# Two buffers instead of one for the layer norm's input and for the output block, in an eight-core transformer kernel

## The chip, the cores and the metric

The kernel runs on the eight cores of one Trainium2 chip. Each core works on 2 of the 16 sequences; no core waits for another or exchanges data with it. The metric is the device time in microseconds (us) of the slowest core. Each core has TensorE (PE; its weight loads are shown apart as PEld), VectorE (DVE), ScalarE (ACT), GpSimd (POOL) and SyncE (SP), which here only issues transfers.

## What is computed

An attention layer with pre-norm, then a feed-forward part that is itself a two-layer transformer with local attention. The edited lines lie in the last part of each of its layers: the norm ahead of `w1`, and the end of the product with `w2`.

```
# x: (16, 2048, 1024) float32
x = x + attention(layernorm(x))
y = layernorm(x)
for l in range(2):
    h = shift_token(y)                       # half of the channels one token later
    y = y + local_attention(h) @ wo[l]
    h = shift_token(y)
    h = (h - mean) / sqrt(var + 1e-5) * ln_g[l] + ln_b[l]     # stage C, first half
    a, g = split(h @ w1[l] + b1[l])                           # stage C, second half
    y = y + (a * gelu(g)) @ w2[l] + b2[l]                     # stage D
x = x + y
```

## The kernel before

A core holds 4096 tokens, channels on the partitions: 8 chunks of 128 channels, and tiles of 512 tokens along the free dimension. The program is a list of operations for each engine (`Sched`). Every operation names the semaphore values for which it waits; `p.v`, `p.s`, `p.t` add an operation to DVE, ScalarE or TensorE, `p.dma` adds a transfer to the queue of SP ("sync"), ScalarE or GpSimd. An engine takes its list strictly in order. `p.fence` hangs further waits on the next operation of the engines that it names, and `p.barrier` makes all engines wait for all that was issued. Every operation of DVE and of ScalarE also waits for the one before it on its engine.

The stages run one after another with a barrier between them: loading and casting weights, attention A for each of the two sequences, then for each of the two FFN layers `l` local attention B, stage C and stage D.

*Stage C* (line 1463 on). Its first half is the layer norm of 8 tiles (`s` is the sequence, `tt` the tile in it). A tile is 8 chunks of 513 float32 columns, loaded from `yB_d` or `yA_d` in HBM into `ytilB` by one transfer of 2052 KB on SP's queue. 513 columns, because the chunks of one half of the channels are read one token earlier (`off`). DVE, ScalarE and TensorE wait for the load by a fence. `emit_ln` (line 391) then casts the 8 chunks to bfloat16 (`lnBxb`, L394), squares them on ScalarE (L397), sums both over the partitions by matmuls with a column of ones (L401, L405), works out mean and factor on one partition (L409 to L430), broadcasts both by two matmuls (L432, L434), and applies them on DVE with three operations for each chunk: two in place in `ytilB` (L440, L450), and one with the layer's scale and offset into `hlnB` (L455). The load of the next tile waits for the last of these, `prev_apply`. Its second half, after the eighth tile, is the product with `w1`: 22 column blocks of the weights (`w1c`, two buffers, loaded on GpSimd's queue, the first two of them at the stage's start), each with 8 tiles of 16 matmuls (L1513, L1519), a GELU on ScalarE, a product on DVE, and one store to `hg_d`.

*Stage D* (line 1548 on). For each of 8 tiles: loads of `hgt`, `ytil2` and, in layer 1, `xat`; 8 x 22 matmuls with `w2` (L1593); DVE adds bias and residual (L1606) into `ynew2`. Layer 0 stores the tile. Layer 1 adds `xat` (L1626) and turns the tile round in four blocks `i` of 128 tokens: 8 transposes on TensorE (L1643) into the PSUM tiles `pA` and `pB`, two copies on DVE (L1649) into `outst`, and one store of 512 KB on SP's queue. `out_dma` is the semaphore value that the last store reaches. Both the transposes of the next block (`wtr`, line 1638 on) and DVE's copies wait for it. On SP's queue the loads of the next tile stand behind the stores of this one.

Of the kernel before, what the change touches and what calls it, by code (L numbers as in the profile page):

```python
# [7 lines left out]
F32 = mybir.dt.float32  # L8
# [244 lines left out]
def build_program(stop=None):  # L253
    stop = stop or DBG_STOP
    nc = bass.Bass("TRN2", target_bir_lowering=False)
    p = Sched()
# [45 lines left out]
    with contextlib.ExitStack() as ctx:  # L302
# [50 lines left out]
        for yd in (yA_d, yB_d):  # L353
            for c in range(8):
                for s in range(SPC):
                    p.dma("sync", yd[c, :, s * (SEQ + 1):s * (SEQ + 1) + 1], zcol,
                          sem="ld1", wait=[("ve", zv)], tag="guard", slow=True)
# [4 lines left out]
        for idx, (src, dstb, nd) in enumerate(  # L362
            [(ew["wqkvA"], wbA_q, 24), (ew["woA"], wbA_o, 8),
             (ew["wqkvB"][0], wbB_q[0], 12), (ew["wqkvB"][1], wbB_q[1], 12)]):
            for k in range(8):
                n = idx * 8 + k
# [4 lines left out]
                            sem="gp0" if n % 2 == 0 else "gp1", wait=w, tag=f"wbc{idx}_{k}")  # L371
# [3 lines left out]
                      sem="ld2" if n % 2 == 0 else "ld3",  # L375
                      wait=[gpt], tag=f"wbs{idx}_{k}"))
# [3 lines left out]
        if stop == "init":  # L380
            p.op("sync", lambda e: e.nop(),
                 wait=[(s, p.now(s)) for s in SEMS if s[0:2] in ("ld", "gp", "sc")], tag="fin")
# [537 lines left out]
        def _layer(l):  # L920
# [40 lines left out]
            for k in range(4):  # L961
                ld_woB = p.dma("gpsimd", woBb[k], ew["woB"][l][k * 128:(k + 1) * 128, :],
                               sem="gp2", tag=f"B{l}wo{k}")
# [13 lines left out]
            for w in range(4):  # L977
# [6 lines left out]
                for i in range(4):  # L984
                    tab_ld = p.dma("gpsimd", tabst[i], ew["tabs"][i][:, w * 1024:(w + 1) * 1024],
                                   sem="gp2", wait=wtab if i == 0 else (), tag=f"B{l}t{w}{i}")
                for s in range(SPC):
# [3 lines left out]
                                 wait=[("ve", ve_all), ("se", se_all)]  # L991
                                 if (w > 0 and s == 0) else (),
                                 tag=f"B{l}y{w}{s}")
                hq_done = None
                for c in range(8):
                    off = 0 if c >= 4 else 1
                    for s in range(SPC):
# [4 lines left out]
                            wait=[ld_y, ("pe", pe_all)] if (c == 0 and s == 0) else (),  # L1002
                            inc=True, tag=f"B{l}h{w}{c}{s}")
                evB = {}
                for d in range(12):
                    buf = wcolB[d % 2]
                    wv = list(wbank_tok)
                    if (d % 2) in mm_doneB:
                        wv.append(("pe", mm_doneB[d % 2]))
                    ld_w = p.dma("sync", buf, wbB_q[l, d], sem="ld2" if d % 2 == 0 else "ld3",  # L1010
                                 wait=wv, tag=f"B{l}w{w}{d}")
                    for s in range(SPC):
                        bank = [pA[:, 0:512], pA[:, 512:1024], pB[:, 0:512],
                                pB[:, 512:1024]][2 * (d % 2) + s]
# [3 lines left out]
                        for k in range(8):  # L1018
# [4 lines left out]
                                wait=wmm if k == 0 else (), inc=(k == 7),  # L1023
                                tag=f"B{l}m{w}_{d}_{s}_{k}")
# [3 lines left out]
                        if d == 0 and s == 0 and w > 0:  # L1028
# [3 lines left out]
                            wait=wevac, inc=True, tag=f"B{l}e{w}_{d}_{s}")  # L1032
# [76 lines left out]
                for c in range(4):  # L1109
                    for s in range(SPC):  # L1110
                        for i in range(4):
                            wv = [("ve", evB[(8 + c, s)])]
                            if vt_hist:
                                wv.append(("ve", vt_hist[-1]))
                            if (c, s, i) == (0, 0, 0) and fin_tokB is not None:
# [5 lines left out]
                                wait=wv, inc=True, tag=f"B{l}vt{w}_{c}{s}{i}")  # L1121
# [6 lines left out]
                                wait=[("pe", pe_t)], inc=True, tag=f"B{l}ve{w}_{c}{s}{i}")  # L1128
                            vt_hist.append(vt_tok)
                vones = None  # L1130
                for i in range(8):
                    vones = p.v(lambda e, i=i, w=w: e.memset(
                        vaugB[w % 2][i].rearrange("p (h x) -> p h x", h=NH_B)[:, :, 64:65], 1.0),
                        wait=[("ve", vt_tok)] if i == 0 else (), inc=True, tag=f"B{l}vo{w}{i}")
# [292 lines left out]
                for s in range(SPC):  # L1427
                    for d in range(8):
                        key = d % 4
                        bank = [pA[:, 0:512], pA[:, 512:1024], pB[:, 0:512],  # L1430
                                pB[:, 512:1024]][key]
# [3 lines left out]
                        for k in range(4):  # L1435
# [4 lines left out]
                                wait=wmm if k == 0 else (), inc=(k == 3),  # L1440
                                tag=f"B{l}wm{w}_{s}{d}_{k}")
                        pe_mm = p.now("pe")
                        wev = [("pe", pe_mm)]
                        if ystore is not None and d < 4:
# [4 lines left out]
                            wait=wev, inc=True, tag=f"B{l}we{w}_{s}{d}")  # L1449
# [5 lines left out]
                          sem="ld7", wait=[("ve", ynew_tok)], tag=f"B{l}ys{w}{s}")  # L1455
# [6 lines left out]

            r2a = Region(nc)
            hlnB = [r2a.sb(f"hlB{c}", [128, T], BF16) for c in range(8)]
            ytilB = r2a.sb("ytilB", [128, 8 * 513], F32)
            ln2 = mk_ln_scratch(r2a, "lnB")
            wcol2 = [r2a.sb(f"w1c{i}", [128, 8 * 256], BF16) for i in range(2)]
            g2st = r2a.sb("g2st", [128, 512], BF16)
            hgst = r2a.sb("hgst", [128, T], BF16)
            p.barrier()  # L1470
            prev_apply = None
            for s in range(SPC):
                for tt in range(4):
                    wv = [("ve", prev_apply)] if prev_apply is not None else []
                    ld_y = p.dma("sync", ytilB.rearrange("p (c j) -> p c j", j=513),
                          p2src[:, :, s * (SEQ + 1) + tt * 512:s * (SEQ + 1) + tt * 512 + 513]
                          .rearrange("c p j -> p c j"), sem="ld5", wait=wv, tag=f"C{l}y{s}{tt}")
                    ints = []
                    for c in range(8):
                        off = 0 if c >= 4 else 1  # L1480
                        ints.append(ytilB[:, c * 513 + off:c * 513 + off + 512])
                    p.fence(("vector", "scalar", "tensor"), {ld_y[0]: ld_y[1]})
                    louts = emit_ln(ln2, ints,
                                    [hlnB[c][:, (s * 4 + tt) * 512:(s * 4 + tt + 1) * 512]
                                     for c in range(8)],
                                    gb=([lng_sb[:, 8 * l + c:8 * l + c + 1] for c in range(8)],
                                        [lnb_sb[:, 8 * l + c:8 * l + c + 1] for c in range(8)]),
                                    tag=f"C{l}n{s}{tt}")
                    prev_apply = louts[-1]
            hln_done = p.now("ve")  # L1490
            w1_mm_done = {}
            prev_hg = None
# [1 line left out]
            for c2 in range(W2C):  # L1494
                buf = wcol2[c2 % 2]
                wv = []
                if (c2 % 2) in w1_mm_done:
# [4 lines left out]
                      sem="gp0" if c2 % 2 == 0 else "gp1", wait=wv, tag=f"C{l}w{c2}")  # L1502
                hg_tok = {}
                for tt8 in range(8):
# [7 lines left out]
                    for k in range(8):  # L1512
# [4 lines left out]
                            wait=wmm if k == 0 else (), tag=f"C{l}a{c2}_{tt8}_{k}")  # L1517
# [10 lines left out]
                    elif prev_hg is not None:  # L1528
# [4 lines left out]
                        wait=wsg, inc=True, tag=f"C{l}gg{c2}_{tt8}")  # L1533
                    whg = [("se", sg)]
                    if tt8 < 2 and c2 > 0 and prev_st is not None:
# [5 lines left out]
                        wait=whg, inc=True, tag=f"C{l}hg{c2}_{tt8}")  # L1541
# [3 lines left out]
                                wait=[("ve", hg_tok[7])], tag=f"C{l}hs{c2}")  # L1545
# [3 lines left out]
            r2b = Region(nc)  # L1549
# [2 lines left out]
            ytil22 = [r2b.sb(f"ytil2{i}", [128, 8 * 513], F32) for i in range(2)]  # L1552
            ynew2 = r2b.sb("ynew2", [128, 8 * 512], F32)
            xat = r2b.sb("xat", [128, 8 * 512], F32)
            outst = r2b.sb("outst", [128, 1024], F32)
            p.barrier()
            for k in range(W2C):
                ld_w2 = p.dma("gpsimd", w2b[k], ew["w2"][l][k * 128:(k + 1) * 128, :],
                              sem="gp2", tag=f"D{l}w{k}")
            out_dma = None  # L1560
            mm_pe_tok = {}
            ev7_tok = {}
            fadd7_tok = {}
            for tt8 in range(8):
                s, tt = tt8 // 4, tt8 % 4
# [3 lines left out]
                wv = [hg_st_tok]  # L1569
                if tt8 >= 2:  # L1570
# [3 lines left out]
                        sem="ld4", wait=wv, tag=f"D{l}h{tt8}")  # L1574
# [4 lines left out]
                            tag=f"D{l}y{tt8}")  # L1579
# [34 lines left out]
                if l == 0:  # L1614
                    p.dma("sync",
                          p2dst[:, :, s * (SEQ + 1) + 1 + tt * 512:s * (SEQ + 1) + 1 + tt * 512 + 512]
                          .rearrange("c p j -> p c j"),
                          ynew2.rearrange("p (c j) -> p c j", j=512),
                          sem="ld7", wait=[("ve", ev2[7])], tag=f"D{l}s{tt8}")
                else:  # L1620
                    fadd = {}
                    for d in range(8):
                        wfa = [("ve", ev2[d])]
                        if d == 0:
                            wfa.append(ld_x2)
                        fadd[d] = p.v(lambda e, d=d: e.tensor_add(  # L1626
                            out=ynew2[:, d * 512:(d + 1) * 512],
                            in0=ynew2[:, d * 512:(d + 1) * 512],
                            in1=xat[:, d * 512:(d + 1) * 512]),
                            wait=wfa, inc=True, tag=f"D{l}fa{tt8}_{d}")  # L1630
                    fadd7_tok[tt8] = fadd[7]
                    for i in range(4):
                        evo = {}
                        for chalf in range(2):
                            bank = pA if chalf == 0 else pB
                            for cc in range(4):
                                c = chalf * 4 + cc
                                wtr = []
                                if cc == 0:
                                    wtr = [("ve", fadd[7])]  # L1640
                                    if out_dma is not None:
                                        wtr.append(out_dma)
                                p.t(lambda e, c=c, cc=cc, i=i, bank=bank: e.transpose(  # L1643
                                    bank[:, cc * 128:(cc + 1) * 128],
                                    ynew2[:, c * 512 + i * 128:c * 512 + (i + 1) * 128],
                                    identf),
                                    wait=wtr, inc=(cc == 3), tag=f"D{l}tr{tt8}_{i}_{c}")
                            pe_tr = p.now("pe")
                            evo[chalf] = p.v(lambda e, chalf=chalf, bank=bank: e.tensor_copy(  # L1649
                                out=outst[:, chalf * 512:(chalf + 1) * 512], in_=bank[:, 0:512]),  # L1650
                                wait=[("pe", pe_tr)] + ([out_dma]
                                                        if out_dma is not None else []),
                                inc=True, tag=f"D{l}te{tt8}_{i}_{chalf}")
                        out_dma = p.dma("sync", out[t0 + i * 128:t0 + (i + 1) * 128, :], outst,
                                        sem="ld7", wait=[("ve", evo[1])], tag=f"D{l}os{tt8}_{i}")
            r2b.close()

            if stop == f"p2_{l}":
# [30 lines left out]
```

How the kernel before makes its waits and increments, by code:

```python
            def body(eng, items=items):  # L130
                waited = {}
                for fn, waits, incs, tag in items:
                    for s, v in waits:
                        if v > 0 and waited.get(s, -1) < v:
                            eng.wait_ge(sems[s], v)
                            waited[s] = v
                    ins = fn(eng)
                    for s, a in incs:
                        ins.then_inc(sems[s], a)
```

## Time and profile before

| | us |
|---|---|
| median of 2 timed runs | 11558.8 |
| the two runs | 11468.06 and 11649.55 |
| profiled execution | 11585.54 |
| its span on the slowest core (4) | 11583.9 |
| its span on the fastest core (3) | 11405.2 |

The span of a core goes from its first to its last instruction. The rows further down are of core 4, unless they name another. "A <- B" in a list of waits says that A's engine was idle until B was done. The granted clock is a share of TensorE's 2.4 GHz; 0.5 is the lower level, 1.2 GHz.

### The profile page before, as it was taken

What the parts mean: (1) busy time and instruction counts of PE and PEld (TensorE: products, weight loads), DVE (VectorE), ACT (ScalarE), POOL (GpSimd) and SP (SyncE); (2) the same over time, 40 slices, a digit from 0 to 9 for tenths busy, and PEclk for the clock granted to TensorE, in tenths of its full rate; (3) what the DMA queues carried; (4) which work ended last, traced back from release to release, by engine and by line L of the source; (5) the groups of instructions that cost most, each with busy time, mean ns of one, the idle gap of its engine ahead of it and who ended that gap; (6) DMA issues with size and microseconds to landing.
All of it is one profiled execution on the core that took longest, in us unless ns stands there. A gap on an engine that the chain in (4) does not pass through costs nothing.

```text
span 11583.9 us, 91738 instructions; the slowest of 8 cores (11405.2 to 11583.9 us)
## 1 busy us (share of the span) xinstructions
PE 7162.2 (62%) x26571; PEld 2809.4 (24%) x26848; DVE 3733.0 (32%) x6382; ACT 2306.4 (20%) x3892; POOL 230.1 (2%) x420
## 2 busy tenths in 40 slices
PE   0667777366777744465663588674564755288665
PEld 0222222122222211122221233221221322033332
DVE  1434333443434333323234311103333233511112
ACT  0023333102333312132221111001221322111000
POOL 0000000000000000000000000000000000000000
PEclk9765555776555575655555788776656555688777
DMA  6100000310000030110101122331101101122332
GB/s 132 49 7 7 8 7 21 109 49 7 7 8 7 21 113 10 43 44 12 50 7 58 38 45 48 103 114 41 50 7 46 32 24 40 45 44 48 72 124 103
DMA packets 363271, 520.59 MB, mean 45 GB/s; under 512 B 87204, under 2 KB 196900, under 8 KB 357156
## 3 DMA queue, kind: packets, MB, share of 16 engines
q1 hardware_dynamic: 266276, 417.92, 10.9%
q0 software_dynamic: 68608, 60.07, 3.6%
q10 hardware_dynamic: 27904, 36.72, 1.5%
q8 instruction: 236, 3.87, 0.1%
q14 instruction: 247, 2.02, 0.1%
HBM read 350.76 MB, written 178.27 MB: 46 GB/s over the span
## 4 chain that ended last, share of the span: by engine, by line
PE 48%; DVE 18%; DMA 13%; ACT 11%; issue 8%; ACTq 1%; DVEq 1%; SPq 0%; POOL 0%; POOLq 0%
PE pE L800 4%; DVE mstA L697 4%; PE pA L1593 3%; DMA hg_d<-hgst 3%; PE pB L1593 3%; ACT ztA L788 3%; PE pA L1513 3%; PE pC L768 3%; PE pA L1519 2%; PE pB L1519 2%; PE pB L1513 2%; PE pE L1367 2%; PE pA L541 2%; DMA hgt<-hg_d 2%; PE pA L1019 2%
## 5 line engine op out<-in xcount | busy, mean ns | idle before, releaser
L788 ACT ACTIVATE ztA<-pC 128x512 bf16<-128x512 f32 (+1 forms) x640 | 355.3, 555 | 1162.2 <-PE pC L768 743.9
L1593 PE MATMUL pA<-hgt,w2b 128*128 128x512 bf16 x1379 | 357.2, 423 | 337.7 <-DMA hgt<-hg_d 218.1
L1513 PE MATMUL pA<-hlB,w1c 128*128 128x512 bf16 x1380 | 407.4, 445 | 190.1 <-DVE hgst L1537 150.9
L825 DVE COPY rbcA<-pFb 64x512 f32<-64x512 f32 x128 | 87.4, 683 | 1356.5 <-PE pFb L822 1356.5
L800 PE MATMUL pE<-ztA,Vg 128*65 128x512 bf16 (+3 forms) x1280 | 452.9, 531 | 0.0
L1393 DVE COPY rbcB<-pFb 64x512 f32<-64x512 f32 x128 | 87.4, 683 | 1098.7 <-PE pFb L1390 1098.7
L768 PE MATMUL pC<-qtlA,ktlA 65*128 65x512 bf16 (+2 forms) x640 | 326.3, 510 | 162.5 <-ACT ztA L788 161.4
L697 DVE TENSOR_REDUCE mstA<-pA 128x1 f32<-128x512 f32 (+3 forms) x640 | 391.5, 612 | 69.1 <-DVE mstA L697 1.6
L697 DVE TENSOR_REDUCE mstA<-pB 128x1 f32<-128x512 f32 (+3 forms) x640 | 391.5, 612 | 68.6 <-DVE mstA L697 1.4
L681 PE MATMUL pA<-KT,QT 64*128 64x512 bf16 (+2 forms) x768 | 306.1, 463 | 171.3 <-DVE mstA L697 161.5
L1537 DVE SCALAR_TENSOR_TENSOR hgst<-pA,c_b,g2st 128x512 bf16<-128x512 f32 x176 | 132.1, 751 | 845.7 <-ACT g2st L1530 494.6
L1019 PE MATMUL pA<-hqB,wcB 128*128 128x512 bf16 x753 | 198.5, 420 | 293.4 <-ACT hqB L998 292.6
L1519 PE MATMUL pA<-hlB,w1c 128*128 128x512 bf16 x1380 | 377.2, 420 | 2.5 <-issue 0.9
L1519 PE MATMUL pB<-hlB,w1c 128*128 128x512 bf16 x1380 | 361.3, 406 | 2.0
L1513 PE MATMUL pB<-hlB,w1c 128*128 128x512 bf16 x1378 | 360.7, 406 | 2.1
L681 PE MATMUL pB<-KT,QT 64*128 64x128 bf16 (+3 forms) x896 | 313.9, 431 | 66.9 <-DVE mstA L697 64.5
L788 ACT ACTIVATE ztA<-pD 128x512 bf16<-128x512 f32 (+2 forms) x640 | 327.9, 512 | 62.7 <-ACT ztA L788 2.8
L1593 PE MATMUL pB<-hgt,w2b 128*128 128x512 bf16 x1378 | 332.5, 401 | 1.9
L401 PE MATMUL pA<-lnBxb,c_onescol 128*1 128x512 bf16 x128 | 68.6, 583 | 422.4 <-DVE lnBxb L394 422.4
L1343 ACT ACTIVATE ztB<-pC 128x128 bf16<-128x128 f32 (+1 forms) x448 | 199.5, 445 | 600.7 <-PE pC L1335 462.4
L768 PE MATMUL pD<-qtlA,ktlA 65*128 65x512 bf16 (+1 forms) x512 | 278.4, 544 | 32.3 <-ACT ztA L788 2.9
L1593 PEld LDWEIGHTS pA<-hgt,w2b 128*128 128x128 bf16 x1408 | 149.0, 107 | 542.8 <-issue 450.7
(262 smaller groups left out, 11392.0 us busy)
## 6 DMA issues: line engine op xcount, KB each, us to landing
hg_d<-hgst SPq DMA_DIRECT2D x44, 1024.0 KB, 8.5
hgt<-hg_d SPq DMA_DIRECT2D x16, 2816.0 KB, 15.8
ytB<-yA_d SPq DMA_DIRECT2D x16, 2052.0 KB, 15.7
ytilB<-yB_d SPq DMA_DIRECT2D x16, 2052.0 KB, 8.6
ytil<-yB_d SPq DMA_DIRECT2D x16, 2052.0 KB, 20.6
yB_d<-ynew SPq DMA_DIRECT2D x16, 2048.0 KB, 8.7
wcB<-wbB_q SPq DMA_DIRECT2D x96, 256.0 KB, 2.6
w1c<-w POOLq DMA_DIRECT2D x44, 512.0 KB, 7.4
```

The costliest lines, as they stand in the source:

```text
L541: p.t(lambda e, tt=tt, k=k, bank=bank, buf=buf: e.matmul(bank, buf[:, k * 128:(k + 1) * 128], hlnA[k][:, tt * 512:(tt + 1) * 512], start=( ...
L681: ch=ch, rbase=rbase, msk=msk: e.matmul(pq[:, off:off + nn], QT[ch][rbase:rbase + 64, qtg * 128:(qtg + 1) * 128], KT[ch][rbase:rbase + 64, ...
L697: single=single: e.reduce_max(out=mst[:, 4 + qt:5 + qt] if single else mst[:, nmst:nmst + 1], in_=pq[:, 0:seg], axis=AX.X, negate=True),
L768: p.t(lambda e, pz=pz, kc=kc, qb=qb, q0=q0, ktl=ktl, qtl=qtl: e.matmul(pz[:, q0 * 128:512], ktl[:, kc * 128:(kc + 1) * 128], qtl[:, qb * 5 ...
L788: exp_tok[kc] = p.s(lambda e, pz=pz, kc=kc, col0=col0: e.activation(out=ztA[kc][:, col0:512], in_=pz[:, col0:512], func=AF.Exp, scale=0.12 ...
L800: p.t(lambda e, kc=kc, h=h, col0=col0: e.matmul(pE[0:65, col0:512], Vaug[kc][:, h * 65:(h + 1) * 65], ztA[kc][:, col0:512], start=(kc == 0 ...
L1019: p.t(lambda e, k=k, bank=bank, buf=buf, s=s: e.matmul(bank, buf[:, k * 128:(k + 1) * 128], hq[k][:, s * 512:(s + 1) * 512], start=(k == 0 ...
L1343: col1=col1: e.activation(out=ztB[kc][:, col0:col1], in_=pz[:, col0:col1], func=AF.Exp, scale=8.0),
L1367: col0=col0, col1=col1, w=w: e.matmul(pE[0:65, col0:col1], vaugB[slot][tile][:, h * 65:(h + 1) * 65], ztB[kc][:, col0:col1], start=(kc == ...
L1513: p.t(lambda e, k=k, buf=buf, tt8=tt8, bka=bka: e.matmul(bka, buf[:, k * 256:k * 256 + 128], hlnB[k][:, tt8 * 512:(tt8 + 1) * 512], start= ...
L1519: p.t(lambda e, k=k, buf=buf, tt8=tt8, bkg=bkg: e.matmul(bkg, buf[:, k * 256 + 128:k * 256 + 256], hlnB[k][:, tt8 * 512:(tt8 + 1) * 512], ...
L1593: p.t(lambda e, k=k, d=d, bank=bank, hgt=hgt: e.matmul(bank, w2b[k][:, d * 128:(d + 1) * 128], hgt[:, k * 512:(k + 1) * 512], start=(k == ...
```

## The change

Two buffers are doubled, in each case with the waits that belong to the buffer itself.

1. Stage C: `ytilB` becomes two buffers, taken in turn by the tile's number `n`. The load of tile `n` waits for the last apply of tile `n - 2` in place of `n - 1`, and the first two loads wait for none. The loads signal on two semaphores in turn, `ld5` and `ld6`.
2. Stage D, layer 1: `outst` becomes two buffers, taken in turn by the block's number `i`. DVE's copy waits for the last store from the same buffer (`od2[i % 2]`) in place of the last store of all. The lines with the transposes' wait, a few lines above, are not in the diff: they still add `out_dma`, which is still the last store.

```diff
-            ytilB = r2a.sb("ytilB", [128, 8 * 513], F32)
+            ytilB2 = [r2a.sb(f"ytilB{i}", [128, 8 * 513], F32) for i in range(2)]
...
-            prev_apply = None
+            apl = {}
             for s in range(SPC):
                 for tt in range(4):
-                    wv = [("ve", prev_apply)] if prev_apply is not None else []
+                    n = s * 4 + tt
+                    ytilB = ytilB2[n % 2]
+                    wv = [("ve", apl[n - 2])] if (n - 2) in apl else []
                     ld_y = p.dma("sync", ytilB.rearrange("p (c j) -> p c j", j=513),
                           p2src[:, :, s * (SEQ + 1) + tt * 512:s * (SEQ + 1) + tt * 512 + 513]
-                          .rearrange("c p j -> p c j"), sem="ld5", wait=wv, tag=f"C{l}y{s}{tt}")
+                          .rearrange("c p j -> p c j"), sem="ld5" if n % 2 == 0 else "ld6",
+                          wait=wv, tag=f"C{l}y{s}{tt}")
...
-                    prev_apply = louts[-1]
+                    apl[n] = louts[-1]
...
-            outst = r2b.sb("outst", [128, 1024], F32)
+            outst2 = [r2b.sb(f"outst{i}", [128, 1024], F32) for i in range(2)]
...
             out_dma = None
+            od2 = {0: None, 1: None}
...
                     for i in range(4):
                         evo = {}
+                        outst = outst2[i % 2]
...
-                                wait=[("pe", pe_tr)] + ([out_dma]
-                                                        if out_dma is not None else []),
+                                wait=[("pe", pe_tr)] + ([od2[i % 2]]
+                                                        if od2[i % 2] is not None else []),
                                 inc=True, tag=f"D{l}te{tt8}_{i}_{chalf}")
                         out_dma = p.dma("sync", out[t0 + i * 128:t0 + (i + 1) * 128, :], outst,
                                         sem="ld7", wait=[("ve", evo[1])], tag=f"D{l}os{tt8}_{i}")
+                        od2[i % 2] = out_dma
```

## Rows read from the trace of the kernel before

**Rows 1.** Spans and mean granted clock of the cores.
```profile
core 0: 11405.7 us, clock 0.660
core 1: 11438.8 us, clock 0.660
...
core 4: 11583.9 us, clock 0.646
```

**Rows 2.** The page, busy time by engine.
```profile
PE 7162.2 (62%) x26571; PEld 2809.4 (24%) x26848; DVE 3733.0 (32%) x6382; ACT 2306.4 (20%) x3892; POOL 230.1 (2%) x420
```

**Rows 3.** View by tile of `ytilB`, both layers: count, ns min/median/max; idle until; landing.
```profile
L440 DVE TENSOR_TENSOR ytilB<-ytilB,pB x128: 686/689/690, 6217.4 to 10098.7; 128x512 f32<-128x512 f32 x128
L70 SPq DMA_DIRECT2D ytilB<-yB_d x16: 359/360/360, 6191.8 to 10059.3; - x16
...
  DMA ytilB<-yB_d: 123.5, 14
...
DMA to landing us min/median/max: 8.2/8.6/10.2
```

**Rows 4.** Timeline of DVE, 6234 to 6249: start, us, engine, operation, [idle before].
```profile
6233.94 0.69 DVE L450 SCALAR_TENSOR_TENSOR ytilB<-pB,ytilB 128x512 f32<-128x512 f32 x1
6234.74 0.55 DVE L455 TENSOR_SCALAR hlB<-ytilB,c_lng,c_lnb 128x512 bf16<-128x512 f32 x1
6244.18 4.15 DVE L394 CAST lnBxb<-ytilB 128x512 bf16<-128x512 f32 x8 [8.89 <-DMA ytilB<-yB_d]
```

**Rows 5.** Waits of SP's queue, 6180 to 6560, and of DVE, 6191 to 6525.
```profile
SPq L135 <- DVE hlB L455: 289.9, 7, 43.1
...
DVE lnBxb L394 <- DMA ytilB<-yB_d: 61.4, 7, 9.1
...
DVE lnBxb L394 <- DMA w1c<-w: 17.7, 1, 17.7
```

**Rows 6.** The chain of waits in order of time, layer 0's stage C: start, us, what.
```profile
6235.37 8.65 DMA ytilB<-yB_d
6244.76 4.31 PE pA L401 x8
...
6290.80 1.95 PE pA L405 x8
...
6413.94 3.43 PE pA L405 x8
...
6526.47 3.19 PE pA L1513 x7
```

**Rows 7.** Engines' busy time in two windows (clock, DMA share, GB/s last); timeline of both tiles' starts.
```profile
6235.30:6244.10 8.80, 0.00 (x0) 0.00 (x0) 0.00 (x0) 0.00 (x0) 0.00 (x0) 0.50 0.68 239
6244.10:6276.80 32.70, 7.79 (x18) 1.64 (x18) 23.05 (x39) 6.40 (x10) 0.00 (x0) 0.55 0.00 1
...
6202.08 4.14 DVE L394 CAST lnBxb<-ytilB 128x512 bf16<-128x512 f32 x8 [17.67 <-DMA w1c<-w]
6244.76 4.31 PE L401 MATMUL pA<-lnBxb,c_onescol 128*1 128x512 bf16 x8 [27.49 <-DVE lnBxb L394]
```

**Rows 8.** View by tile of `outst`: idle until; who waited for it.
```profile
  PE pA L1643: 112.6, 32
...
  PE pA L1643: 89.6, 24
```

**Rows 9.** Timeline of TensorE, two blocks of the first output tile.
```profile
10996.65 1.08 PE L1643 MATMUL pA<-c_identf,ynew 128*128 128x128 f32 x4 [3.72 <-DMA out<-outst]
...
11002.31 1.09 PE L1643 MATMUL pA<-c_identf,ynew 128*128 128x128 f32 x4 [3.72 <-DMA out<-outst]
```

**Rows 10.** Transfers issued from 7402 to 7430: KB each, us to landing.
```profile
hgt<-hg_d SPq DMA_DIRECT2D x1, 2816.0 KB, 16.5
ytil<-yB_d SPq DMA_DIRECT2D x1, 2052.0 KB, 21.3
yA_d<-ynew SPq DMA_DIRECT2D x1, 2048.0 KB, 9.4
```

**Rows 11.** Groups by line of TensorE, layer 0's layer norm, 6191 to 6525.
```profile
L405 PE MATMUL pA<-lnBsq,c_onescol 128*1 128x512 bf16 x64 | 21.4, 492 | 0.0
```

**Rows 12.** View by line L1513, first of core 0, then of core 4.
```profile
L1513 PE MATMUL pA<-hlB,w1c x1408: 376/379/634, 6499.2 to 10714.8; 128*128 128x512 bf16 x176
...
L1513 PE MATMUL pA<-hlB,w1c x1380: 376/435/634, 6526.5 to 10876.5; 128*128 128x512 bf16 x198
```

**Rows 13.** Two windows of the first FFN matmuls, core 4 (columns as in rows 7).
```profile
6542.00:6660.00 118.00, 103.77 (x440) 45.34 (x448) 21.03 (x28) 19.26 (x28) 2.64 (x3) 0.94 0.19 41
6660.00:6821.00 161.00, 146.74 (x544) 60.32 (x554) 26.28 (x35) 24.08 (x35) 4.38 (x5) 0.80 0.21 47
```

More of the change, by code:

```diff
@@ L1648, in _layer @@
                             pe_tr = p.now("pe")
-                            evo[chalf] = p.v(lambda e, chalf=chalf, bank=bank: e.tensor_copy(
+                            evo[chalf] = p.v(lambda e, chalf=chalf, bank=bank,
+                                             outst=outst: e.tensor_copy(
                                 out=outst[:, chalf * 512:(chalf + 1) * 512], in_=bank[:, 0:512]),
-                                wait=[("pe", pe_tr)] + ([out_dma]
-                                                        if out_dma is not None else []),
+                                wait=[("pe", pe_tr)] + ([od2[i % 2]]
+                                                        if od2[i % 2] is not None else []),
                                 inc=True, tag=f"D{l}te{tt8}_{i}_{chalf}")
```

## The prediction, made before the changed kernel was run

> **What bounds the kernel now.** I read the spans and granted clocks of the cores first [rows 1]: the slowest core, 4, ends at 11583.9 us, the fastest at 11405.2. No core waits for another in this program, so a saving counts where the slowest core has it. Busy time comes next [rows 2]: TensorE is busy for 62% of the span and no other engine for more than 32%, so no single engine is full; the kernel is a row of stages, and what an edit is worth is read inside its stage. Both edited places are short stages in which engines take turns.
>
> The first is the layer norm ahead of the first FFN matmuls (line 1468 on; 8 tiles in each of the two layers). The view by tile of `ytilB` [rows 3] shows what the stage consists of: 128 casts, 3 x 128 applying operations on DVE, 16 loads of 2052 KB, and DVE idle for 123.5 us in 14 places until such a load lands. The timeline of DVE at one change of tile [rows 4] shows the place itself: the last operation of a tile starts at 6234.74 and takes 0.55, the next tile's first cast starts at 6244.18, 8.89 us later. The waits of the layer's stage [rows 5] say why the load is late: SP held it until DVE had finished with the tile (289.9 us in 7 waits). The chain of waits [rows 6] runs through this load, then the cast, then the statistics matmuls, so the 8.9 us lie on the path; in the stretch 6235.3 to 6244.1 nothing computes on any engine [rows 7].
>
> The second place is the end of the last stage, where the result is transposed and stored in 32 blocks of 128 rows (line 1632 on). There the view by tile of `outst` [rows 8] shows TensorE idle for 89.6 us, 24 times, until a store has landed, while DVE's copies wait for TensorE's transposes (112.6 us) and for no store. In the timeline [rows 9] a block takes 5.7 us (transposes at 10996.65, then at 11002.31), of which 3.72 is TensorE waiting for the store.
>
> **Edit 1, two `ytilB` buffers.** Removed: the wait of load n for the last apply of tile n-1. It now waits for tile n-2. The first two loads of each layer go out at once; load n+1 goes out when tile n-1 is done, so it has the whole of tile n for its transfer. From the first cast of one tile (6202.08) to that of the next (6244.18) are 42.10 us [rows 4, 7], of which 8.89 are the wait and 33.2 the tile's own work. The load takes 8.2 to 10.2 us [rows 3]. It is hidden behind 33 us, and would have to become over three times as long to show. On SP nothing stands between these loads, so none is held by something else.
>
> How many waits go: 7 changes of tile in a layer, 14 in all, which is the count of the row. Their idle is 123.5 us [rows 3]. What stays of each is the normal step from one DVE operation to the next, 0.11 us (6233.94 + 0.69 to 6234.74 [rows 4]), 14 x 0.11 = 1.5. Gain: 123.5 - 1.5 = 122.0 us. The first load of each layer still shows in full (17.7 us in the first layer, put down to `w1c`, a transfer issued with it [rows 5]).
>
> Costs of this edit that the trace does not show directly:
> - The second load now stands behind the first at the start of a layer. Lower bound 0: the same queue is served roughly in order, since of a 2816 KB and a 2052 KB load issued together in the last stage, behind a store of 2048 KB, the store landed after 9.4 us, the larger load after 16.5 and the smaller, issued last, after 21.3 [rows 10]. Upper bound: the two share evenly and the first lands when the second does, one load later, 8.6 us a layer, 17 in all. I take 0, as in that row the earlier one was hardly held up.
> - A load now runs beside DVE's work. The eight casts of the first tile, during which `w1c` was still arriving, took 4.14 us, those of the next, with no transfer, 4.15 [rows 4, 7]. So 0; were the whole of each transfer to slow DVE by a tenth, it would be 14 x 8.6 x 0.1 = 12 us. A layer has this at most.
> - TensorE's granted clock during the statistics. Eight L405 matmuls took between 1.93 and 3.43 us in different tiles [rows 6], at a mean clock of 0.55, mostly the 1.2 GHz level [rows 7], and 21.4 us over 8 tiles, 2.7 each [rows 11]. TensorE's pause between tiles gets 8.8 us shorter, from 27.5 [rows 7], so which level a tile meets can change: at most 16 x 0.75 = 12 us either way. I take 0.
> - The loads' second semaphore, and the shift of buffers in SBUF: 0; DVE, ScalarE and TensorE wait for one semaphore per tile as before.
>
> The Trainium skill (DMA: Bandwidth & Descriptors, Anatomy of one DMA) gives a transfer about 2.0 us plus its bytes at 436 GB/s. By that the load would be an estimated 6.8 us and 14 of them 95 us. The rows have 8.2 to 10.2 us, so the page's figure is too short here, and the measured wait decides.
>
> **Edit 2, two `outst` buffers.** What changes is only the semaphore value for which DVE's copy waits: the store before last instead of the last. But the transposes keep `wtr.append(out_dma)`, and `out_dma` is still the last store. So TensorE waits for the last store, and DVE's copy waits for those transposes; the copy's own wait was always already satisfied. The 3.72 us per block stays, 24 times. Gain 0, loss 0 (a few satisfied waits fewer on DVE). Were TensorE freed as well, it would be the full 89.6 us, the other bound.
>
> **Sum.** Against the profiled execution: 11585.5 - 122.0 + 0 = 11463.5 us. The two timed runs of before are 11649.6 and 11468.1, median 11558.8, which is 26.7 below the profiled time. The same saving on the median gives 11436.8; I state 11440. That is 1.1%.
>
> **What moves the time more than the edit.** Core 4 has the same work as core 0 and ends 178 us later. From its first to its last L1513 matmul core 0 takes 4215.6 us (6499.2 to 10714.8), core 4 4350.0 (6526.5 to 10876.5), 134.4 more [rows 12]. The windows [rows 13] show a granted clock of 0.94 (nearly all at 2.4 GHz) in one dense stretch of the FFN's first matmuls on core 4, and 0.80 in the next, on the same code, with TensorE busy throughout both. This comes from execution to execution and from die to die, and is why the runs of before lie 181 us apart. The edit leaves the dense matmuls as they are. The Trainium skill (TensorE: Matmul & The Clock Gate, Part 1) tells of a limit of 13/16 of the full clock on a die once three of its cores run dense matmuls. Core 4's 0.80 agrees, core 0's die did not show it in the same execution, so it is not a constant that the sum could use.
>
> **Rivals.**
> - *The stores are freed too* (edit 2 pays): for it, the name of the buffer and the 89.6 us of idle; against it, the transposes' wait, which the diff leaves. It would give 11440 - 90 = 11350. Chance 0.03.
> - *The load does not get hidden*: the wait for tile n would also have to wait for load n+1, or the transfer would have to grow past 33 us. The two semaphores are separate and the row's longest load is 10.2 us, so there is little for it. It gives the median of before, 11559. A half-way form is the sharing above with all costs at their bounds, 17 + 12 + 12, giving 11480. Together 0.07.
> - *Slower than before*: the lower clock holds for longer on the slowest core. Its place is the four dense FFN stages, its price so far 178 us on core 4 for the stretches that it had. It decides when it costs a further 122 us, that is, when the low stretches grow by about two thirds; twice as much gives 11440 + 178 = 11618. For it: less idle ahead of the dense stages; against it: the idle taken away is 122 us of 11584, and lies between tiles of the layer norm, where the clock is at 0.55 [rows 7] and TensorE does little before as well as after. Chance 0.04.
> - *The lower clock is absent on all cores*: core 1, the slowest of the undisturbed die, had 11438.8 [rows 1], and 11438.8 - 122 = 11317. Chance 0.06.
>
> **How the numbers follow.** The forecast case has 0.80. Its own spread is that of the runs of before moved by 122: 11346 to 11528. I take the range from 11330 to 11540: below it reaches toward the undisturbed case, above it takes in part of the 41 us of unknown costs. A measurement of this kernel tells about 2% from no change, and 2% of 11558.8 is 231 us, nearly twice the saving. Faster by over 2% needs the saving and another 109 us: 0.06. Slower by over 2% needs over 350 us of lost clock: 0.01. Within 2%: 0.93.
>
> **What the changed profile would show.** DVE's idle until `ytilB` loads land falls from 123.5 us to none but the first of each layer; tiles follow each other every 33.3 us (33.2 and the step of 0.11) instead of 42.1; the stage from the first cast to the first L1513 matmul falls from 324.4 us (6202.08 to 6526.47 [rows 6]) to about 264; the eight loads are issued one tile ahead. In the last stage TensorE still waits 24 times, 89.6 us, for the store. The dense stages keep their length apart from the clock. I would be wrong if a load under way stretches DVE's operations beyond 0.69 us, if the first load lands much later than 10.2 us, or if the 24 waits on the stores go.

## The result

The changed kernel takes 11465.2 us, the median of 27 runs (11335.0 to 11676.9); beside it the kernel before took 11594.7, the median of 26 (11441.5 to 11814.1). The ratio is 0.989, with a 95% interval of 0.985 to 0.993: 1.1% less time, clear of noise, and within 2%. The forecast was 11440 us, rounded from the earlier median of 11558.8 less 122.0. The median of the kernel before over 26 runs is 36 us above that of its first two; the forecast saving taken from the new median gives 11472.7.

The profile after was taken while one die's granted clock was lower in the dense stages, so spans must be compared between dies with an undisturbed clock, die 0 of before (median of its cores 11421.8 us) and die 1 of after (11316.9), 105 us less. The spans and granted clocks of the cores after:

```profile
core 3: 11495.6 us, clock 0.642
core 4: 11336.8 us, clock 0.660
...
die 0 (median of its cores): 11437.5 us, clock 0.647
die 1 (median of its cores): 11316.9 us, clock 0.661
```

A sharper measure is the length of each stage on each core. The norm is counted from its first cast to the first w1 matmul, w1 from its first matmul to the start of its last (L1519, L1522 after), and w2 from its first matmul to the start of its last or, in layer 1, to the issue of the last store. The norm's numbers are medians over all eight cores, the others over the cores whose clock was not disturbed in that stage. They are worked out from the starts in the traces, in us:

| kernel | norm, layer 0 / 1 | w1, layer 0 / 1 | w2, layer 0 / 1 |
|---|---|---|---|
| before | 323.7 / 321.2 | 736 / 742 | 446 / 626 |
| after | 262.3 / 262.1 | 735 / 742 | 446 / 625 |

The norm lost 61.3 and 59.1 us, 120.4 together, and the other stages kept their length. The view by tile of `ytilB` after (core 3) answers to [rows 3]; the lines are one of the operations, what DVE waited for, and the landing times:

```profile
L440 DVE TENSOR_TENSOR ytilB<-ytilB,pB x128: 686/689/691, 6223.0 to 9989.0; 128x512 f32<-128x512 f32 x128
...
  DMA ytilB<-yB_d: 36.7, 2
...
DMA to landing us min/median/max: 8.3/9.5/20.0
```

Fourteen places with 123.5 us of idle have become two with 36.7, the first load of each layer. Those two were there before as well, 17.7 us put down to `w1c` in layer 0 [rows 5] and 17.5 in layer 1. The applying operation takes 689 ns, as before; the load that is now hidden runs beside the casts ahead of it, which start 14 us sooner, and has landed (9.6 us in the median) before this operation starts. The timeline of DVE after, at the first change of tile, answers to [rows 4]:

```profile
6208.63 4.14 DVE L394 CAST lnBxb<-ytilB 128x512 bf16<-128x512 f32 x8 [17.43 <-DMA ytilB<-yB_d]
...
6240.26 0.55 DVE L455 TENSOR_SCALAR hlB<-ytilB,c_lng,c_lnb 128x512 bf16<-128x512 f32 x1
6240.91 4.14 DVE L394 CAST lnBxb<-ytilB 128x512 bf16<-128x512 f32 x8
```

The next tile's casts start 0.10 us after the last apply ends, where there were 8.89 us, and its eight casts take 4.14 us beside the load, as they did without one (4.15). Over the layer the tiles follow each other every 32.3 to 33.7 us. The view by tile of `outst` after answers to [rows 8], the timeline of TensorE to [rows 9]:

```profile
  PE pA L1648: 112.4, 32
...
  PE pA L1648: 89.6, 24
```
```profile
10897.76 1.09 PE L1648 MATMUL pA<-c_identf,ynew 128*128 128x128 f32 x4 [3.73 <-DMA out<-outst]
10903.43 1.08 PE L1648 MATMUL pA<-c_identf,ynew 128*128 128x128 f32 x4 [3.73 <-DMA out<-outst]
```

The same 24 waits, 89.6 us, and a block still takes 5.67 us: the second output buffer has changed nothing.

### The profile page after: what moved, and what is told of

Its sections match the earlier page's. It is cut to its first block, busy times and chain, and to the rows that moved or that the text cites. A ratio compares the mean times of both kernels' runs of the same rounds, so it can differ in the third digit from the quotient of the medians.

```text
span 11495.6 us, 92009 instructions; the slowest of 8 cores (11286.7 to 11495.6 us)
## 1 busy us (share of the span) xinstructions
PE 7252.9 (63%) x26848; PEld 2820.5 (25%) x26848; DVE 3732.7 (32%) x6382; ACT 2307.2 (20%) x3892; POOL 229.3 (2%) x420
## 4 chain that ended last, share of the span: by engine, by line
PE 49%; DVE 18%; DMA 12%; ACT 11%; issue 8%; DVEq 1%; ACTq 1%; SPq 0%; POOL 0%; POOLq 0%
PE pE L800 4%; DVE mstA L697 4%; PE pA L1597 3%; DMA hg_d<-hgst 3%; PE pB L1597 3%; PE pA L1516 3%; ACT ztA L788 3%; PE pC L768 3%; PE pA L1522 2%; PE pB L1522 2%; PE pB L1516 2%; PE pE L1367 2%; PE pA L1019 2%; PE pA L541 2%; DMA hgt<-hg_d 2%
## 5 line engine op out<-in xcount | busy, mean ns | idle before, releaser
L1597 PE MATMUL pA<-hgt,w2b 128*128 128x512 bf16 x1408 | 358.3, 421 | 322.4 <-DMA hgt<-hg_d 217.9
L1516 PE MATMUL pA<-hlB,w1c 128*128 128x512 bf16 x1408 | 421.1, 453 | 188.9 <-DVE hgst L1540 152.5
L1522 PE MATMUL pA<-hlB,w1c 128*128 128x512 bf16 x1408 | 388.9, 426 | 0.0
L1522 PE MATMUL pB<-hlB,w1c 128*128 128x512 bf16 x1408 | 371.9, 412 | 0.0
L1540 DVE SCALAR_TENSOR_TENSOR hgst<-pB,c_b,g2st 128x512 bf16<-128x512 f32 x176 | 132.1, 751 | 463.2 <-ACT g2st L1533 463.2
```

Of the source, the lines that this page charges most:

```text
L1516: p.t(lambda e, k=k, buf=buf, tt8=tt8, bka=bka: e.matmul(bka, buf[:, k * 256:k * 256 + 128], hlnB[k][:, tt8 * 512:(tt8 + 1) * 512], start= ...
L1522: p.t(lambda e, k=k, buf=buf, tt8=tt8, bkg=bkg: e.matmul(bkg, buf[:, k * 256 + 128:k * 256 + 256], hlnB[k][:, tt8 * 512:(tt8 + 1) * 512], ...
L1540: hg_tok[tt8] = p.v(lambda e, bka=bka, c2=c2, tt8=tt8: e.scalar_tensor_tensor(out=hgst[:, tt8 * 512:(tt8 + 1) * 512], in0=bka, scalar=b1_s ...
L1597: p.t(lambda e, k=k, d=d, bank=bank, hgt=hgt: e.matmul(bank, w2b[k][:, d * 128:(d + 1) * 128], hgt[:, k * 512:(k + 1) * 512], start=(k == ...
```

## The experiments

### One edit at a time

`c_only` has the edit of `ytilB` alone, `d_only` that of `outst` alone.

> Only the two ytilB buffers, outst as before. Theory A (the whole gain is the hidden load of the layer norm's tiles): the ratio to the kernel before is that of the full change, about 0.989, and DVE's idle until ytilB loads land falls from some 123 to 145 us (14 or 15 places) to about 36 (the first load of each layer). Rival B (the second outst buffer gives part of it): this kernel gains less than the full change, ratio about 0.997, if the 90 us of store waits were part of the gain.

> Only the two outst buffers, ytilB as before. Theory A: ratio 1.000, TensorE (pA L1643, or its shifted line) waits 24 times, 89 us in all, for out<-outst, and a block of 128 tokens still takes 5.66 us, as the transposes still wait for the last store. Rival B: the waits shrink and the time falls by up to 90 us, ratio 0.992.

`c_only` measured a ratio of 0.989 (0.980 to 0.999), `d_only` 1.004 (0.996 to 1.011). In `c_only` the two norms take 262.4 us each; in `d_only` they take 323.8 and 323.0, and its last stage 625 us, like the kernel before. The lines of the waits, for `ytilB` in `c_only`, then for `outst` in `d_only`:

```profile
  DMA ytilB<-yB_d: 35.0, 2
```
```profile
  PE pA L1645: 112.5, 32
...
  PE pA L1645: 89.6, 24
```

The intervals of the two ratios overlap a little; the stages do not. The whole gain is the norm's, and the rival in which the second `outst` buffer pays has fallen.

### What keeps the second output buffer from working

`freed_one` takes `c_only` and lets the transposes of block i wait for DVE's copies of block i-1, which free their PSUM bank, in place of its store. There is one `outst` buffer, so DVE's copy waits for the store. `freed_two` is the full change with the same edit, its stores signalling on two semaphores in turn.

```diff
+                    prev_evo = None
                     for i in range(4):
...
-                                    if out_dma is not None:
-                                        wtr.append(out_dma)
+                                    if prev_evo is not None:
+                                        wtr.append(("ve", prev_evo[chalf]))
...
+                        prev_evo = evo
```

> The two ytilB buffers, one outst buffer, and the transposes wait for DVE's copies of the block before in place of its store (DVE's copy still waits for the store). Theory A: the store's landing is then what DVE waits for, so only the first transposes (about 1.1 to 1.4 us a block) move beside it: a block takes about 4.4 us in place of 5.66, 24 x 1.3 = 30 us less in stage D than with the full change. Rival C (the wait on TensorE is the whole cost): a block falls to about 2 us, 85 us less.

> The full change with the transposes waiting for DVE's copies of the block before in place of its store, two outst buffers, the stores on two semaphores in turn. Theory A: now the second buffer counts: a block takes about 2.0 to 2.4 us (two copies of 0.69 us on DVE, eight transposes of 1.75 us on TensorE), 24 x 3.4 = 80 us less than the full change, ratio to before about 0.982. Rival D (another wait takes its place, the next tile's hgt load, which stands behind the stores on SP's queue): the blocks get shorter but the time moves by under 30 us, ratio about 0.987.

The timeline of TensorE, first transposes of consecutive blocks, in `freed_one` and then in `freed_two`:

```profile
10940.81 1.09 PE L1647 MATMUL pA<-c_identf,ynew 128*128 128x128 f32 x4 [0.16 <-DVE outst L1653]
10945.22 0.72 PE L1647 MATMUL pA<-c_identf,ynew 128*128 128x128 f32 x4 [2.47 <-DVE outst L1653]
10949.57 1.09 PE L1647 MATMUL pA<-c_identf,ynew 128*128 128x128 f32 x4 [2.62 <-DVE outst L1653]
```
```profile
10913.09 1.09 PE L1651 MATMUL pA<-c_identf,ynew 128*128 128x128 f32 x4 [0.16 <-DVE outst L1658]
10915.19 0.98 PE L1651 MATMUL pA<-c_identf,ynew 128*128 128x128 f32 x4 [0.16 <-DVE outst L1658]
10917.50 0.72 PE L1651 MATMUL pA<-c_identf,ynew 128*128 128x128 f32 x4 [0.73 <-DVE outst L1658]
```

Blocks follow each other every 4.35 to 4.41 us with one buffer (10945.22 to 10949.57 is 4.35) and every 2.1 to 2.3 with two, against 5.67. The last stage falls from 625 us to 592.5 and to 539.5, 33 and 86 us less; 30 and 80 were expected. The ratios are 0.989 (0.974 to 1.004) and 0.978 (0.968 to 0.987). So with the transposes' wait gone the second buffer is worth 53 us; with the wait in place it was worth nothing. Rival C falls, since a block in `freed_one` still takes 4.35 us or more, and rival D by the stage and by the unchanged wait for `hgt` (221.6 us in 14 places, 217.9 in the profile after).

### How much cover a tile gives

In `load3` and `load5` each load of tiles 2 to 7 is made three or five times, one after another, all but the last into a spare buffer.

```diff
+                    for rp in range(3 if n >= 2 else 1):
+                        last = n < 2 or rp == 2
-                    ld_y = p.dma("sync", ytilB.rearrange(...), ..., wait=wv, ...)
+                        ld_y = p.dma("sync", (ytilB if last else ytilX).rearrange(...), ..., wait=wv, ...)
+                        wv = [ld_y]
```

> The two ytilB buffers alone, and each load of tiles 2 to 7 made three times, one after the other (twice into a spare buffer, the third time into its own): three transfers of 2052 KB, about 9 us each, 27 us, between the end of tile n-2 and the start of tile n. Theory A (a tile gives 33 us of cover and a transfer beside DVE costs DVE nothing): the layer norm stays at 262 us from its first cast to the first w1 matmul. Rival E (a transfer slows DVE beside it, at least by a tenth): six tiles get 2.7 us longer, 278 us or more.

> As load3, with five transfers in a row, 43 to 47 us, more than the 33 us of a tile. Theory A (the cover is one tile's own work): the loads now set the pace from tile 2 on: 33.3 for tile 0, six times 43 to 47, 33.3 for tile 7, so 325 to 349 us in place of 262. Rival F (the cover is larger, two tiles, since there are two buffers): the stage stays near 262.

With three transfers the norm takes 262.5 us (the median of 16 norms, 261.3 to 263.1; the changed kernel's 16 have 262.2), with five 326.1 to 335.0. The transfers issued in one norm, `load3` (KB each, us to landing), and its engines in 200 us of it (DMA's busy share and GB/s stand last):

```profile
ytilX<-yB_d SPq DMA_DIRECT2D x12, 2052.0 KB, 8.8
ytilB<-yB_d SPq DMA_DIRECT2D x6, 2052.0 KB, 8.8
```
```profile
6240.00:6440.00 200.00, 49.42 (x114) 10.17 (x113) 140.44 (x240) 40.61 (x64) 0.00 (x0) 0.57 0.55 190
```

The DMA engines are busy for 0.55 of the time at 190 GB/s, and the norm has not become longer: a transfer costs DVE nothing that can be measured here, and rival E, which asked for 278 us, falls. Here the transfers run beside the applying operations too, and `ytilB` L440 still takes 689 ns. At five the transfers set the pace, and the cover is one tile's own work, not two. The changed kernel uses 9.6 of some 33 us, the median landing time of its six covered loads in layer 0 (core 3; the loads of the kernel before had 8.6).

### The same question at the next buffers

After `freed_two` two waits on single transfers remained. `hg_two` adds a second `hgst`, the staging buffer whose store to `hg_d` held DVE's product in the w1 stage. `all_ahead` adds to it that the loads of tile t+1 in the w2 stage are issued at the start of tile t, ahead of its stores on SP's queue, each pair with semaphores of its own. Since TensorE then no longer waits for a load at the start of a tile, its first matmuls there wait for DVE's last reading of their PSUM banks (`bank_free`).

```diff
-                    if tt8 < 2 and c2 > 0 and prev_st is not None:
-                        whg.append(prev_st)
+                    if tt8 < 2 and st2[c2 % 2] is not None:
+                        whg.append(st2[c2 % 2])
```
```diff
+                ld_hgt, ld_y2 = tile_ld[tt8]
...
+                if tt8 < 7:
+                    load_tile(tt8 + 1)
```

> freed_two, with two buffers also for hgst, the staging buffer of the w1 stage, so that DVE's product no longer waits for the store of the column block before (42 waits of 8.4 us, 351 to 367 us of idle DVE, but only some 150 us of idle TensorE). Theory G (what TensorE waits is what counts): the w1 stages fall from 736 and 741 us on an undisturbed core to about 665 each, time 140 us below freed_two, ratio about 0.966. Rival H (the denser matmuls are paid back by a lower granted clock): the stages fall on undisturbed cores, but the mean ratio stays above 0.974.

> hg_two, and in the last stage the loads of the next tile are issued at the start of a tile, ahead of its stores on SP's queue, with semaphores of their own; TensorE waited 218 us in 14 places for these hgt loads. Theory G: the w2 stages fall from 446 and 540 us to about 345 and 440, ratio about 0.948. Rival H (the clock takes back a part): a ratio above 0.955, with the stage shorter by 100 us only on cores whose clock is undisturbed.

| kernel | w1, layer 0 / 1 | w2, layer 0 / 1 | ratio to before |
|---|---|---|---|
| `freed_two` | 736 / 741 | 446 / 540 | 0.978 |
| `hg_two` | 609 / 609 | 446 / 540 | median 11108.6 us of 4 runs, no interval |
| `all_ahead` | 609 / 610 | 314 / 502 | 0.947 (0.941 to 0.954) |
| `xat_behind` | 609 / 610 | 315 / 450 | 0.938 (0.927 to 0.948) |

`hg_two` beat theory G: w1 lost 127 us in layer 0, not 71. TensorE writes into the PSUM bank that DVE's product reads, so while the store holds the product, it holds the next matmuls too. The waits and the timeline of TensorE in `freed_two`, core 2, in the w1 stage of layer 0, show where the rest lay:

```profile
PE pA L1516 <- DVE hgst L1540: 91.5, 20, 6.3
```
```profile
6507.41 3.19 PE L1516 MATMUL pA<-hlB,w1c 128*128 128x512 bf16 x8 [4.49 <-DVE hgst L1540]
6510.40 2.31 PE L1522 MATMUL pA<-hlB,w1c 128*128 128x512 bf16 x8
6512.54 1.89 PE L1516 MATMUL pB<-hlB,w1c 128*128 128x512 bf16 x8
6514.27 1.89 PE L1522 MATMUL pB<-hlB,w1c 128*128 128x512 bf16 x8
6516.00 1.89 PE L1516 MATMUL pA<-hlB,w1c 128*128 128x512 bf16 x8
```

After 4.49 us of waiting, the first 16 matmuls take 5.13 us (6507.41 to 6512.54); the next 16 take 3.46. The windows of that place, the wait, the 16 matmuls behind it and the 22 us after them, give the reason (the granted clock is the third number from the end):

```profile
6502.90:6507.40 4.50, 0.02 (x1) 0.02 (x1) 0.75 (x1) 0.00 (x0) 0.00 (x0) 1.00 0.44 179
6507.40:6512.50 5.10, 5.09 (x16) 1.96 (x17) 0.75 (x1) 0.69 (x1) 0.00 (x0) 0.67 0.01 3
6512.50:6534.90 22.40, 22.40 (x105) 10.19 (x104) 4.51 (x6) 4.82 (x7) 0.88 (x1) 1.00 0.14 15
```

The matmuls behind the wait ran at a mean clock of 0.67, so mostly at the 1.2 GHz level, and the later ones at 1.00. The wait costs itself and another 1.7 us. The same reading at the other places of the stage on this core: of the twenty waits one is of 0.2 us, one of 3.18 us lost nothing behind it, and the other 18, of 4.4 to 6.3 us, lost 1.6 to 2.7 us each in their next 16 matmuls, 32 us in all. That gives 91.5 + 32 = 123.5 us, against the 127 measured. The windows of the same core, `freed_two` and then `hg_two`, over a longer stretch, agree:

```profile
6480.00:7050.00 570.00, 493.04 (x2155) 215.55 (x2152) 100.70 (x135) 92.27 (x134) 14.91 (x17) 0.95 0.23 48
```
```profile
6480.00:7050.00 570.00, 567.26 (x2591) 258.43 (x2641) 123.88 (x165) 113.43 (x165) 17.49 (x20) 1.00 0.27 58
```

Rival H, that denser matmuls would be paid back by a lower clock, falls by its numbers: the clock rose to 1.00 in this stretch, the w1 stage of layer 0 took 608.6 to 609.6 us on all eight cores, and the ratio of the medians is 0.958, where H asked for more than 0.974. The denser stage is not safe from the low clock, though. In layer 1 of the same execution two cores took 618 and 627 us, and in the profile of `all_ahead` cores 2 and 3 took 691 and 693 us for w1 in layer 1, at 0.80 over 400 us on core 2, where the others took 609 to 610. The Trainium skill (TensorE: Matmul & The Clock Gate, Part 1) has a limit of 13/16 of the clock once three cores of a die run dense matmuls. Stretches at 0.81 do appear in some executions and on some dies; but in `hg_two` all eight cores ran these matmuls at once, in layer 0, at 0.97 to 1.00 over 300 us, so here the limit did not always set in.

`all_ahead` met the forecast in ratio, but not stage by stage: layer 0's w2 fell to 314 us, below the 345 expected, and layer 1's only to 502, not 440. The expectation had shared the saving out evenly; on core 2 of `freed_two` 125.5 us of the waits for `hgt` lie in layer 0. The queue of SP and the waits of DVE in its last stage (core 4) show a new wait:

```profile
10369.42 0.36 SPq L70 DMA_DIRECT2D xat<-xa_d  x1
10372.36 12.93 SPq L70 DMA_DIRECT2D out<-outst  x4
```
```profile
DVE outst L1680 <- DMA out<-outst: 50.4, 8, 7.5
```

The four stores stood behind a 2048 KB load issued 3 us before them. `xat_behind` moves that load behind the stores:

```diff
                     fadd7_tok[tt8] = fadd[7]
-                    if tt8 < 7:
-                        load_xat(tt8 + 1)
...
                         bank_free = evo[1]
+                    if tt8 < 7:
+                        load_xat(tt8 + 1)
```

> all_ahead, with the load of xat for the next tile issued behind this tile's four stores on SP's queue, as in the kernel before, and no longer ahead of them. Theory X (in all_ahead the 2048 KB load stood ahead of the stores, whose landing the copies of blocks 2 and 3 wait for: 50 us in 8 waits of DVE): this wait goes, the last stage falls from about 500 to about 450 us, ratio about 0.943. Rival Y (the stores were late for another reason, such as the next tile's hgt and ytil2 loads in flight): the stage stays near 500 us and the ratio at 0.947.

The stage fell to 450 us, and the waits of DVE on the stores (core 2) to

```profile
DVE outst L1678 <- DMA out<-outst: 10.5, 12, 2.6
```

so rival Y has fallen too. At 10897.4 us (the median of 6 runs) beside 11620.9 for the kernel before, this version takes 6.2% less time than the kernel before and beats the changed one as well. What the place of `xat`'s load cost is the 52 us of the stage; the whole time can't show it as clearly, since the intervals of the last two ratios overlap.

## Why the prediction was right

- *The gain of edit 1, 122.0 us.* Right: the norms lost 120.4 us, and the count of 14 waits held. The 8.89 us at a change of tile became 0.10, the step of 0.11 that the sum left in place.
- *The stage at about 264 us.* It takes 262.3. The forecast started from core 4's 324.4 us, and the median core had 323.7; a little more came from the statistics, since DVE waited 26.1 us for the L405 matmuls in layer 0 (core 3 after) where it had waited 27.0 (core 4 before). The forecast step of 33.3 us from tile to tile was worked out from one tile; the steps measured range from 32.3 to 33.7.
- *The first load behind a second one, 0 to 17 us.* 0 was right within some 2 us: on core 3 DVE waits 17.4 us for it in layer 0 and 19.3 in layer 1 (36.7 in all), against 17.7 before. The transfers issued in that stretch after the change, which answer to [rows 10] in kind:

```profile
ytilB<-yB_d SPq DMA_DIRECT2D x2, 2052.0 KB, 14.2
yB_d<-ynew SPq DMA_DIRECT2D x1, 2048.0 KB, 7.0
w1c<-w POOLq DMA_DIRECT2D x2, 512.0 KB, 16.5
```

  The chain of waits has the first of the two landing after 9.89 us, where the first load took 10.2 before. The second, issued with it, took some 18.5 us (the 14.2 is the median of the two), so they were served one after the other. Neither it nor `w1c` was waited for.
- *A load beside DVE, 0 to 12 us.* 0, and by `load3` still 0 with three times the traffic; the prediction had reached it from eight casts alone. The Trainium skill (SBUF — State Buffer, SBUF: two separate sides) says that DMA and engines use separate ports and cannot slow each other. The row of `load3` agrees.
- *Edit 2 at nothing.* Right, and for the reason given. `d_only` shows the nothing, `freed_two` shows that the transposes' wait was its cause.
- *The time itself.* 11440 against 11465: the saving was right and the base moved, since the median of the kernel before over 26 runs is 36 us above that of the first two. That it moved no further is luck: those two lay 181 us apart, more than the whole saving. The spread from run to run (before 373 us, after 342) is about twice what the two shown runs had let the prediction expect, and three times the saving. It goes with the granted clock: over the 29 executions of the changed kernel whose cores were recorded, a core's span and its mean clock correlate at -0.96, and core 3 of the profile after has w1 stages of 793.6 and 798.9 us, cores 4 to 7 some 735 and 742.
- *The rivals.* The load was hidden, the stores were not freed, and no loss of clock ate the gain. One price among them was too high: the 178 us between cores 4 and 0 were put into the four dense FFN stages, and by stage these differ by 43 + 34 + 40 + 12, some 128 us. Nothing in the sum rested on it.

## What to carry to other kernels

A second buffer pays only when every engine that waits for the transfer is released, not only the one that touches the buffer: look for the same token in the waits of the instructions ahead of it. The gain of hiding a load is the sum of the waits in the row, and the cover is the work of one tile; a copy of the load in a spare buffer measures how much of that is left. When a wait of TensorE between dense matmuls is priced, add what the first matmuls after it lose, here 1.7 us on 4.5. A load issued ahead of small stores on one queue can hold them up: the stores here landed after up to 9.4 us in `all_ahead` (core 4), and in the kernel before after 3.5 at most.

## What the runs showed of the hardware

- A wait of 4.5 us in a dense stretch of matmuls cost 6.2 us, since the 16 matmuls behind it took 5.13 us in place of 3.46. Taking the 91.5 us of such waits out of a stage of 736 us shortened it by 127, 35 more than the waits themselves.
- Three transfers of 8.8 us beside each 33 us tile of DVE work, at 190 GB/s, changed the stage by nothing that can be measured (262.5 us with three transfers, 262.2 with one).
- In `hg_two` the w1 stage of layer 0 had a mean clock of 1.00 over 570 us on core 2 and took 609 us on all eight cores, while in other executions of these kernels the low clock made a w1 stage take 794 us in place of 735 (the changed kernel, core 3, 0.84 over 300 us of it) or 691 in place of 609 (`all_ahead`, core 2, 0.80 over 400 us). What decides between the two was not found.
